# Retention layer with a routed feed-forward on one core: the order ahead of the first step rewritten, and each tile's outputs spread over three places between expert products

## The reference

```python
x = x + retention(layernorm(x), Wq, Wk, Wv, Wo)   # 8 heads of 16, chunks of 64, state carried over the chunks
x = x + moe(layernorm(x), Wg, W1, W2)             # 8 experts, top 2 of them weighted, hidden 256
...
attn = einsum('bhid,bhjd->bhij', qc, kc) * D                       # scores within a chunk, decayed
o = einsum('bhij,bhje->bhie', attn, vc) + einsum('bhid,bhde->bhie', qc * decay_q, S)
S = decay_s * S + einsum('bhjd,bhje->bhde', kc * decay_k, vc)
...
h = square(relu(einsum('td,edh->teh', xt, W1)))
out = einsum('te,ted->td', combine, einsum('teh,ehd->ted', h, W2)) # combine is 0 but for the chosen two
```

## Time and profile before

| | us |
|---|---|
| median of three runs | 292.0 |
| profiled execution | 291.62 |
| its span | 289.8 |
| PE busy | 273.2 (94%) |
| DVE busy | 220.3 (76%) |
| POOL busy | 197.5 (68%) |
| ACT busy | 178.9 (62%) |

### The profile page before, as it was taken

The page is one execution under the profiler, slowest core; times in us unless marked ns, Lnnn a source line. Parts: engine busy times, 40 slices in busy tenths (PEclk is TensorE's granted clock), DMA queues, the critical chain, the costliest instruction groups (busy, mean ns, idle before and its releaser), DMA issues.

```text
span 289.8 us, 8920 instructions
## 1 busy us (share of the span) xinstructions
PE 273.2 (94%) x3660; PEld 216.6 (75%) x3660; DVE 220.3 (76%) x569; ACT 178.9 (62%) x259; POOL 197.5 (68%) x158
## 2 busy tenths in 40 slices
PE   7988699799999999988999999999999998999995
PEld 5575368578887788767887788778887787878883
DVE  3768559896669956995569967698569849898883
ACT  3517259635976559635675549756675565585961
POOL 1113877899578958796487986789587774465752
PEclk9999799999999999999999999999999999999999
DMA  7239063005140422303141150303230060305301
GB/s 231 80 97 307 7 249 115 3 5 155 65 148 2 124 100 74 110 5 147 75 136 48 39 182 4 111 2 152 72 110 3 6 209 19 104 13 207 109 2 72
DMA packets 13721, 26.80 MB, mean 92 GB/s; under 512 B 1136, under 2 KB 6768, under 8 KB 13680
## 3 DMA queue, kind: packets, MB, share of 16 engines
q1 hardware_dynamic: 13680, 26.23, 27.8%
HBM read 24.00 MB, written 2.23 MB: 90 GB/s over the span
## 4 chain that ended last, share of the span: by engine, by line
POOL 39%; issue 26%; PE 25%; DVE 5%; ACT 4%; POOLq 1%; DVEq 0%; ACTq 0%
POOL act_lo L1186 35%; POOL rstd L1146 3%; PE h_ps L381 2%; PE bank L554 2%; PE h_ps L382 2%; PE h_ps L383 2%; PE y_ps L409 2%; PE y_ps L403 2%; PE bank L565 2%; PE y_ps L404 2%; DVE attn L739 1%; POOL xt_lo L1171 1%; PE y_ps L355 1%; PE bank L578 1%; ACT act_hi L1054 1%
## 5 line engine op out<-in xcount | busy, mean ns | idle before, releaser
L1186 POOL TENSOR_TENSOR act_lo<-act_sf,act_hi 128x512 fp32r<-128x512 f32 x112 | 150.3, 1363 | 52.6 <-ACT act_sf L1061 52.3
L859 DVE SCALAR_TENSOR_TENSOR act_sf<-h_ps,scale 128x1024 f32<-128x1024 f32 x64 | 77.9, 1218 | 44.3 <-issue 21.2
L1054 ACT ACTIVATE act_hi<-act_sf 128x1024 fp32r<-128x1024 f32 x64 | 68.3, 1067 | 53.7 <-DVE act_sf L859 53.6
L1061 ACT ACTIVATE act_sf<-act_sf 128x1024 f32<-128x1024 f32 x64 | 67.6, 1056 | 0.0
L381 PE MATMUL h_ps<-x_hi,w_lo 128*128 128x512 f32 x128 | 53.1, 415 | 0.8 <-DVE attn L739 0.8
L382 PE MATMUL h_ps<-x_lo,w_hi 128*128 128x512 f32 x128 | 50.5, 395 | 0.0
L383 PE MATMUL h_ps<-x_hi,w_hi 128*128 128x512 f32 x128 | 50.5, 394 | 0.0
L403 PE MATMUL y_ps<-act_hi,w_lo 128*128 128x512 f32 x112 | 47.1, 420 | 0.0
L404 PE MATMUL y_ps<-act_hi,w_hi 128*128 128x512 f32 x112 | 44.1, 394 | 0.0
L409 PE MATMUL y_ps<-act_lo,w_hi 128*128 128x512 f32 x112 | 35.2, 396 | 0.1
L381 PEld LDWEIGHTS h_ps<-x_hi,w_lo 128*128 128x128 f32 x128 | 24.1, 188 | 9.5 <-issue 3.0
(11 more groups left out here) (155 smaller groups left out, 434.8 us busy)
## 6 DMA issues: line engine op xcount, KB each, us to landing
scale<-scratch SPq DMA_DIRECT2D x32, 512.0 KB, 4.0
x_t_in<-x_tr SPq DMA_DIRECT2D x8, 256.0 KB, 5.1
x_all<-x SPq DMA_DIRECT2D x8, 256.0 KB, 5.1
out<-out_sb SPq DMA_DIRECT2D x8, 256.0 KB, 4.2
scale<-w SPq DMA_DIRECT2D x1, 768.0 KB, 5.6
cst<-constants SPq DMA_DIRECT2D x1, 288.0 KB, 4.9
cst<-constants SPq DMA_DIRECT2D x1, 256.0 KB, 2.7
scale<-w SPq DMA_DIRECT2D x1, 256.0 KB, 5.7
```

The costliest lines, as they stand in the source:

```text
L859: nc.vector.scalar_tensor_tensor(out=act_s[:, u % 2], in0=h_ps[:, u % 2], scalar=0.0, in1=scale[:, f % 2, e].unsqueeze(1).to_broadcast([P, ...
L1054: nc.scalar.activation(act_hi[:, u % 4], act_s[:, u % 2], ACT.Square).then_inc(act_hi_ready, 1)
L1061: nc.scalar.activation(act_f[:, u % 2], act_s[:, u % 2], ACT.Square).then_inc(act_f_ready, 1)
L1186: nc.gpsimd.tensor_tensor(act_lo[:, u % 4, n], act_f[:, u % 2, n], act_hi[:, u % 4, n].bitcast(F32), ALU.subtract).then_inc(pool_low_ready, 1)
```

## The change

**Ahead of step 0.** PE projects v and transposes k of tile 1 ahead of the outputs of tile 0; `scores(1)` stand behind `project_out(0)` and take other banks; the centering of the last two weight pieces comes ahead of tile 1's outputs, and both first `w1_product`s come behind them. ACT makes all high pieces ahead of `high_second`, which stands behind `copy_roots(0)`. DVE and POOL are reordered to match; DVE's `mask_updates(1)` now stands behind `choose(0)` and `decay_scores(1, (3,))`. Several waits go away or change with the banks.

**In step 0.** DVE does the decay masks of three pairs of tile 2 ahead of `choose(1)` (before: one, then `choose(1)`, then two). POOL takes the root of tile 1's variance ahead of `low(1)` in place of behind it.

**In every step with a tile a.** `outputs_within` is cut in halves at slots 13 and 14, `outputs_before` goes from slot 14 to 15, and ACT's `copy_o(a)` from ahead of the eighth expert's `square` to behind it. In step 6 `route` goes from slot 4 to 5.

```diff
@@ -193,11 +193,11 @@
             if s == 0:
                 return (b0[1], b1[1], center_bank[0], center_bank[1])[pair]
             if s == 1:
-                return (center_bank[0], center_bank[1], b2[1], b0[0])[pair]
+                return (b1[1], b2[1], b0[1], b0[0])[pair]
             return (h_ps[:, LENT % 2, HALVES - 1], b1[0], b2[0], b0[0])[pair]
         def chunk_bank(s, c):
-            return (b2[0], b0[0])[c] if s == 1 else (b1[0], b2[0])[c]
+            return (b1, b2)[c][buffers(s)]
         def router_bank(s):
             return b2[0] if s == 0 else late_bank
@@ -361,19 +361,18 @@
                 if u == 0:
                     pe.wait_ge(x_hi_ready, 1)
                     pe.wait_ge(x_lo_ready, 1)
-                    pe.wait_ge(k_d_ready, 2)
-                    pe.wait_ge(v_z_ready, 2)
                 elif u == 1:
-                    pe.wait_ge(attn_ready, PAIRS + 3)
-                    pe.wait_ge(piece_whole, 4)
+                    pe.wait_ge(piece_whole, PIECES)
                 else:
                     if e == 0:
                         pe.wait_ge(x_hi_ready, f + 1)
                         pe.wait_ge(x_lo_ready, f + 1)
                     pe.wait_ge(act_s_ready, u - 1)
                 for n in range(HALVES):
+                    if u == 0 and n == HALVES - 1:
+                        pe.wait_ge(o_t_ready, 2)
                     if e == LENT and n == HALVES - 1 and f + AHEAD + 1 < TILES:
                         pe.wait_ge(attn_ready, PAIRS * (f + AHEAD + 1) + 1)
                     cols = slice(n * P, (n + 1) * P)
@@ -422,14 +420,8 @@
                     pe.wait_ge(w1_pair_loaded, DMA)
                 elif i == 2:
                     pe.wait_ge(w1_loaded, DMA)
-                if i < 2:
-                    pe.wait_ge(attn_ready, PAIRS + i + 1)
-                else:
+                if i >= 2:
                     pe.wait_ge(piece_whole, i - 1)
-                if i == 4:
-                    pe.wait_ge(root_t_ready, 1)
                 whole = wg_in if i == 0 else w1_in[:, 2 * i - 2:2 * i].rearrange("p e h -> p (e h)")
                 pe.matmul(center_bank[i % 2][:, 0:whole.shape[1]], cst[:, C_CENTER:C_CENTER + P], whole,
                           start=True, stop=True).then_inc(piece_done, 1)
@@ -493,17 +485,12 @@
             def scores(s):
                 b = buffers(s)
                 pe.wait_ge(q_m_ready, s + 1)
-                if s == 1:
-                    pe.wait_ge(attn_ready, PAIRS)
-                    pe.wait_ge(k_d_ready, 1)
-                    pe.wait_ge(q_d_ready, 2)
-                    pe.wait_ge(k_t_ready, 2)
-                elif s >= 2:
+                if s >= 1:
                     pe.wait_ge(k_d_ready, s + 1)
                     pe.wait_ge(v_z_ready, s + 1)
                     pe.wait_ge(q_d_ready, s + 1)
+                if s >= 2:
                     pe.wait_ge(logit_sum_ready, s)
                     pe.wait_ge(act_s_ready, EXPERTS * (s - AHEAD - 1) + LENT - 1)
@@ -542,11 +523,11 @@
                                              stop=(g == GROUPS - 1), skip_group_check=True)
                 last.then_inc(u_done, 1)
-            def outputs_within(s):
+            def outputs_within(s, groups=range(GROUPS)):
                 b = buffers(s)
                 pe.wait_ge(attn_ready, PAIRS * (s + 1))
                 pe.wait_ge(update_ready, 2 * (s + 1))
-                for g in range(GROUPS):
+                for g in groups:
                     for j in range(2):
                         for pair in range(PAIRS):
                             for c in range(2):
@@ -622,7 +602,7 @@
                         project_out(p)
                     if n == (2 if f >= 1 else 0):
                         transpose_x2(p)
-                    if n == (6 if f == 0 else 5 if a < TILES else 4):
+                    if n == (6 if f == 0 else 5):
                         route(p)
                     if n == 13:
                         transpose_roots(p)
@@ -639,8 +619,10 @@
                     if n == 11:
                         state_updates(a)
                     if n == 13:
-                        outputs_within(a)
+                        outputs_within(a, (0, 1))
                     if n == 14:
+                        outputs_within(a, (2, 3))
+                    if n == 15:
                         outputs_before(a)
             pe.wait_ge(zeroed, 1)
@@ -654,26 +636,27 @@
             project_q(1)
             state_updates(0)
             project_k(1)
+            project_v(1)
+            transpose_k(1)
             outputs_within(0)
             outputs_before(0)
+            center_piece(0)
+            project_out(0)
             scores(1)
-            project_out(0)
-            project_v(1)
-            transpose_k(1)
-            center_piece(0)
             transpose_x2(0)
             center_piece(1)
             route(0)
             center_piece(2)
             state_updates(1)
+            center_piece(3)
+            center_piece(4)
+            outputs_within(1, (0, 1))
+            transpose_roots(0)
+            outputs_within(1, (2, 3))
+            outputs_before(1)
             w1_product(0, 0)
-            outputs_within(1)
-            center_piece(3)
-            transpose_roots(0)
-            outputs_before(1)
             project_out(1)
             w1_product(0, 1)
-            center_piece(4)
             for f in range(TILES):
                 for e in range(EXPERTS):
                     if EXPERTS * f + e >= 2:
@@ -894,18 +877,19 @@
             dve.wait_ge(third_loaded, DMA)
             mask_updates(0)
             scan_states(0)
+            statistics(1, 0)
             decay_q(1)
-            statistics(1, 0)
-            decay_scores(1, (0, 1))
+            decay_k(1)
             add_attention(0)
             statistics(0, 1)
+            decay_scores(1, (0,))
+            low_x(0)
+            decay_scores(1, (1,))
+            shift_logits(0)
             decay_scores(1, (2,))
-            low_x(0)
-            decay_k(1)
+            choose(0)
             decay_scores(1, (3,))
-            shift_logits(0)
             mask_updates(1)
-            choose(0)
             spread_roots(0)
             scan_states(1)
             statistics(2, 0)
@@ -938,9 +922,13 @@
                 scale_h(f, 4)
                 low(u + 3)
                 if a < TILES:
-                    decay_scores(a, (0,))
-                    choose(p)
-                    decay_scores(a, (1, 2))
+                    if f == 0:
+                        decay_scores(a, (0, 1, 2))
+                        choose(p)
+                    else:
+                        decay_scores(a, (0,))
+                        choose(p)
+                        decay_scores(a, (1, 2))
                 if p < TILES <= a:
                     spread_roots(p)
                 scale_h(f, 5)
@@ -1088,11 +1076,11 @@
             keep_x(0)
             exponentiate(0)
             high_piece(2)
+            high_piece(3)
+            high_piece(4)
+            copy_roots(0)
             high_second()
-            copy_roots(0)
-            high_piece(3)
             copy_o(1)
-            high_piece(4)
             for f in range(TILES):
                 a, p, u = f + AHEAD + 1, f + AHEAD, EXPERTS * f
                 if f == 0:
@@ -1132,9 +1120,9 @@
                 if p < TILES:
                     copy_roots(p)
                 square(u + 6)
+                square(u + 7)
                 if a < TILES:
                     copy_o(a)
-                square(u + 7)
         @block.gpsimd
         def _(pool):
@@ -1199,17 +1187,19 @@
             pool.wait_ge(combine_ready, 1)
             low_piece(2)
-            low_second()
             low_piece(3)
             low_piece(4)
+            low_second()
             root_variance(2, 0)
             for f in range(TILES):
                 a, p, u = f + AHEAD + 1, f + AHEAD, EXPERTS * f
                 if f >= 1:
                     low(u - 1)
                 low(u)
+                if f == 0:
+                    root_variance(p, 1)
                 low(u + 1)
-                if p < TILES:
+                if f >= 1 and p < TILES:
                     root_variance(p, 1)
                 low(u + 2)
                 if p < TILES <= a:
```

19 lines of the change are left out of this document (7 added, 12 removed).

## The result

The changed kernel takes 293.88 us (median of 20 runs, 290.94 to 296.96) against 292.19 for the kernel before (20 runs beside it, 289.09 to 295.52). The ratio is **1.0072, interval 1.0042 to 1.0103**: 0.7% slower, inside the 2%, with the whole interval above 1. (All ratios here leave out executions over 1.5% above the fastest of the same kernel, so they are not the quotients of the medians.) The forecast was 286.7 with a range of 283.5 to 291.0, so the prediction is wrong, by 7 us and in direction.

The account below looks back on a forecast made before the run. The prediction took a step to be as long as PE's own list plus PE's idle time. Its terms, -2.4 - 1.6 - 2.7 + 1.1 + 1.5 - 0.8 = -4.9, led from 291.6 to 286.7 us, range 283.5 to 291.0.

Parts of the forecast that it names:

- start: Ahead of step 0: the third first product starts at 39.9 in place of 42.3, -2.4 us.
- step 0: In step 0: PE's waits of 0.83 and 1.66 for masks go, partly given back by later updates; -1.6 us.
- gaps: PE stops inside small products at instruction packet ends; halving the outputs shrinks the large gap and three small ones, -2.7 us.
- third place: One more switch between first products and small products, 0.19 each in six steps, +1.1 us.
- copy behind the square: Steps 0 to 4: project_out on PE waits some 0.3 for ACT's later copy of the outputs, +1.5 us.
- route of step 6: Step 6: the route's 0.74 wait for ACT's copy of x goes when it stands one second product later, -0.8 us.
- the 3.1 us: Ahead of step 0: copy of tile 0's roots ends at about 32.0 in place of 35.1, 3.1 earlier.
- The prediction's 39.9: Ahead of step 0: time when PE's own list, last to arrive, lets the third first product start, before 42.3.
- The updates are masked some 1.4 after PE has reached tile 2's outputs: Step 0: the choice moves behind the masks, delaying roots and masked updates; takes 1.4 from the 2.5 won.
- the rival of the head start given back: Step 0: DVE may be the bound once PE stops waiting for one of its results; 289.7 us, chance 0.13.
- The rule with 3.3 us from the packet's first instruction: Gaps: a packet needs an estimated 3.3 us; 250 records used up faster stall PE; halves leave 0.5 of the large gap.

Follow-up runs that it names:

- the filler: Changed kernel with 13 dummy products of 128 columns on PE around the transpose of tile 1's roots in step 0; 293.21 us, ratio 1.0043.
- three places alone: Kernel before with only the outputs in three places and the copy behind the eighth square; 292.54 us, ratio 1.0066.
- 64 waits: Kernel before with 64 more wait instructions on PE behind the first dummy products; 298.88 us, ratio 1.0236.
- 16 and 32 waits: Two kernels: kernel before, later step 6 route, 16 or 32 PE wait instructions ahead of tile 0's route; 291.75 us (0.9991) and 291.87 us (1.0022).
- the two parts alone: Kernel before with tile 4's outputs, in step 2 only, in three places and step 6's route one second product later; 289.56 us, ratio 0.9929.
- the start alone: Changed kernel with the pieces of all steps put back, leaving only the new order ahead of step 0 and its banks; 292.88 us, ratio 1.0004.
- the early root: Kernel before with POOL's root of tile 1's variance ahead of low(1) and step 6's route one second product later; 291.94 us, ratio 0.9993.

## Why the prediction was wrong, step by step

| step | predicted | measured |
|---|---|---|
| start | -2.4 | +0.3 (alone, 1.0004; in two traces where the clock held, -2.1 and -2.4) |
| step 0 | -1.6 | +2.7 (-2.6 + 5.7 - 0.4) |
| gaps | -2.7 | -2.8 (steps 2, 3, 5: 2.0, 0.3, 0.5) |
| third place | +1.1 | +2.3 (6 x 0.39) |
| copy behind the square | +1.5 | +1.1 (4 x 0.28; in step 0 hidden behind the waits) |
| route of step 6 | -0.8 | -0.9 |

**Start: this step failed, for want of a term for the clock.** I walked DVE's and PE's lists with the same lengths and let the end of the roots pass straight into the scaling. Three things took the 3.1 us. The roots are ready at 33.84, 0.2 later than before in relation to tile 0's `state_updates`, not 0.3 earlier. The last two weight pieces ran at the lower clock level (2.07 and 1.69 us for two matmuls each), the transpose stood behind them and waited 0.47 more for ACT's part of them, so that the copy was 1.2 earlier relative to that mark, not 3.1. And SP's loads follow its store by 2.86 us in place of 1.44:

```profile
36.02 0.35 SPq L298 DMA_DIRECT2D scratch<-combine_t  x1
38.88 1.77 SPq L314 DMA_DIRECT2D scale<-scratch  x4
```

The scaling starts at 43.26, 29.7 behind the mark as against 29.4. Other steps of these two traces have 1.4 to 3.5 between store and loads.

Two experiments with this same start show what it gives when the clock holds, first the old mask order, then the filler (from tile 0's `state_updates` to the third first product):

```profile
13.61:42.23 28.62, 23.90 (x650) 17.24 (x650) 20.32 (x81) 12.69 (x28) 13.42 (x12) 1.00 0.52 153
```

```profile
11.64:40.01 28.37, 23.88 (x651) 17.22 (x650) 20.55 (x81) 12.71 (x28) 13.42 (x12) 1.00 0.53 158
```

The prediction's 39.9 is 28.4 behind that mark. So the walk itself was sound: the pieces took 1.12 and 1.02, the loads followed the store by 1.43, and PE's own list was the last to arrive, without a wait, so that 2.1 and 2.4 were won on the kernel before. In the other three traces with the new start (31.0, 31.4 and 31.4) the clock fell for 3.4 us at the weight pieces and the loads followed by 2.9 to 3.0. Up to the pieces the profiled execution and the one with the old mask order run alike, to 0.05 us; why the clock fell in one stays open, and so does what made the loads late. The old order varies too, from 29.3 to 30.8 over eight traces, so that the gain over it is at most 2.4 and often none.

**Step 0: this step failed, and in this pair of traces it decided the sign of the sum.** "The updates are masked some 1.4 after PE has reached tile 2's outputs" stood for waits of 2.9. The walk took DVE's small operations at 0.2, while the trace before already had one of them at 1.20 beside POOL's `low`. Moving the choice behind the masks put the whole chain of share, POOL's root, `spread`, `combine_r` and the update's copy beside a full POOL. That is the rival of the head start given back, with the wrong price: 289.7 had no term for the clock. The three traces with the new order and its two waits (the changed kernel, the one with the copy ahead, step 0's orders alone: 1.3 to 2.2, then 1.5) have a fall of 6.8 us each, the one with the filler none. But the old order is not free of it: behind its 0.8 to 1.0 and then 1.7 the clock held in three traces (before, three places alone, 64 waits) and fell for 3.4 us in three (16 and 32 waits, the two parts alone). Behind a single wait it fell after 1.67 (the start alone) and 2.81 (the early root), and held after 2.68 (the old mask order). So the fall is a risk of a wait and not its fixed price. Without any it would not have been enough either: the two executions of the changed kernel whose mean clock was 1.00 took 290.94 and 292.30 us, not 286.7.

**Gaps: right in place and in sum, the rule half right.** They fall on the ends of packets, as the counts said, and the shifts of 16, 32 and 64 instructions moved them record by record. The Trainium skill's "Runtime: NRT & Kernel Launch", section "Instruction fetch mechanics", has the crossing "mostly hidden"; every trace here differs, with a gap of 1.22 us or more in tile 0's outputs, and seven of the thirteen have another of 1.8 to 2.2. The rule with 3.3 us from the packet's first instruction gave the right 0.5 for the halves (0.34 and 0.36 measured; in the last kernel the second half took 1.06 in place of 0.86, so 0.2) and failed for a product at the packet's head. The sum holds: step 2 takes 0.33 more than its neighbours (33.50 to 33.17) in place of 2.28 (34.80 to 32.52), `outputs_before` of step 5 takes 1.16 in place of 1.67, and step 3 grew by 0.37 where its neighbours grew by 0.65.

**Third place: mechanism right, size off.** 0.19 came from the one product between `outputs_within` and `outputs_before`. Measured it is 0.39 per place: the product between the halves takes 1.60, the second half 0.79 as if it were a run of its own (0.79 + 0.79 against 1.41), and the product ahead of `outputs_before` now has a run on one side more. Six of them are worth 1.2 us more than predicted.

**Copy and route: right.** The copy cost 0.28 in four steps where 0.3 in five was forecast; in the changed kernel it shows in the length of the steps, not as a wait that the trace names.

With the measured terms the sum is 0.3 + 2.7 - 2.8 + 2.3 + 1.1 - 0.9 = +2.7. The profiled spans differ by 2.5 behind tile 0's `state_updates` (4.6 less 2.1), the medians by 1.7; of the 2.7, 2.4 are the clock in step 0 of this one execution, more than it costs on average. Of the 7.6 between this sum and the forecast's -4.9, step 0 holds 4.3, the start 2.7 and the third place 1.2.

## What to carry to other kernels

A wait that goes away in a hand-ordered kernel is worth what the next one on the same list leaves of it: walk the whole chain of the engine that feeds PE, with each operation's length taken beside the work that will run next to it. A cost per step, even of 0.3 us, outweighs a gain that stands in one place; make such a change only in the step that needs it. A profile is one execution: compare the granted clock of the two stretches before a difference between them is put down to the change. Of six parts, the two that won were worth 0.7% alone, and lost 0.7% together with the other four.

## What the runs showed of the hardware that was not expected

- **Some of DVE's small operations last until POOL's running instruction ends.** With POOL idle, 4 to 64 columns in SBUF take 0.15 to 0.25 us. Beside POOL they took as long as was left of its instruction: in the kernel before 0.54 with 0.49 left, 1.11 with 1.09 left, 1.20 with 1.13 left. `spread` took 0.22 there since POOL's piece ended 0.12 behind its start, and 1.31 in the changed kernel, where a piece had just begun. MAX8, FIND_INDEX8, TENSOR_REDUCE (0.14 to 0.22) and the decay masks (0.68), which read PSUM, kept their length. In the kernel with the old mask order a cast of 8 columns, at 55.45 beside POOL's `low`, took 1.31. The Trainium skill, "GPSIMD Engine Reference", section "Specifications", names contention of the two for DVE's instructions with two SBUF inputs or in a 2-port mode; the trace agrees for `spread` and `combine_r`. The copy and the cast have one input, and whether they ran in such a mode no trace shows.
- **An instruction that only waits, for something long done, costs PE 0.06 us** (64 in 3.62, and 32 in 1.75 ahead of the route).
- **A packet of instructions that is used up fast costs up to 2.2 us**, and the fetch begins about 1 us after the run of small products did, however much of the packet came before (two traces).
- **Between 2.4 and 1.2 GHz** a handful of microseconds are at stake in one execution: the 20 executions of the changed kernel had mean clocks from 0.98 to 1.00; the nine up to 0.982 took 293.72 to 296.96, the two at 1.00 took 290.94 and 292.30.
